# Two of the turns in an attention step leave TensorE: gated values by way of DRAM, exponentials by sixteen small DMAs, each finished by a VectorE transpose

## What is computed

```python
z = cumlogsumexp(s, axis=time)
g = exp(z_prev - z); p = exp(s - z)
hk = hk * g + k[:, None] * p                 # per token, key state
ok = q @ hk                                  # 64 scores of a token and head
pv = softmax(ok)
hv = hv * g[:, None] + p[:, None] * v        # value state
o  = pv @ hv                                 # 128 values of a token and head
o  = o * rsqrt(mean(o*o) + 1e-5) * g_norm_weight
o  = o * (gate * sigmoid(gate))              # the gated values
y  = o.reshape(b, t, VALUE_DIM) @ Wo
```

## Time and profile before

| | |
|---|---|
| time, median of 3 runs | 1524.1 us (1523.93 to 1524.8) |
| the profiled execution | 1523.6 us; its span from first to last instruction 1521.8 us |
| TensorE matmul | 1490.4 us busy, 98% |
| VectorE | 1030.9 us busy, 68% |
| ScalarE, GpSimd | 654.6 us (43%), 432.4 us (28%) |
| granted TensorE clock, mean | 0.997 of full speed |
| DMA | 121.17 MB, mean 80 GB/s; packets under 2 KB 75136 of 108016 |

### The profile page before, as it was taken

The page is one execution under the profiler, slowest core; times in us unless marked ns, Lnnn a source line. Parts: engine busy times, 40 slices in busy tenths (PEclk is TensorE's granted clock), DMA queues, the critical chain, the costliest instruction groups (busy, mean ns, idle before and its releaser), DMA issues.

```text
span 1521.8 us, 24247 instructions
## 1 busy us (share of the span) xinstructions
PE 1490.4 (98%) x9586; PEld 1207.6 (79%) x9586; DVE 1030.9 (68%) x1992; ACT 654.6 (43%) x1249; POOL 432.4 (28%) x282
## 2 busy tenths in 40 slices
PE   8999999999999999999999999999999898999998
PEld 6888888888888888888888888878878655666676
DVE  5666655665556666655666577777777776877788
ACT  5333333333323333333443333334333357677675
POOL 0211011210204344433454433122331333333320
PEclk9999999999999999999999999999999999999999
DMA  4421111110202121222223311101200315444553
GB/s 154 167 63 56 42 49 56 58 67 29 75 17 69 60 82 63 83 70 70 84 85 98 88 53 49 47 25 39 63 30 27 111 70 171 127 132 132 160 168 97
DMA packets 108016, 121.17 MB, mean 80 GB/s; under 512 B 5376, under 2 KB 75136, under 8 KB 107904
## 3 DMA queue, kind: packets, MB, share of 16 engines
q1 hardware_dynamic: 103920, 113.07, 23.5%
q10 hardware_dynamic: 3984, 6.56, 1.2%
HBM read 92.34 MB, written 27.26 MB: 79 GB/s over the span
## 4 chain that ended last, share of the span: by engine, by line
PE 92%; DVE 4%; issue 1%; ACT 1%; POOL 1%; DMA 0%; POOLq 0%; DVEq 0%; ACTq 0%
PE bank L457 19%; PE bank L463 18%; PE bank L460 18%; PE bank L686 6%; PE bank L583 4%; PE bank L701 4%; PE bank L722 3%; PE bank L545 2%; PE bank L518 2%; PE bank L591 2%; PE bank L569 2%; PE bank L526 1%; PE bank L540 1%; PE bank L533 1%; PE bank L577 1%
## 5 line engine op out<-in xcount | busy, mean ns | idle before, releaser
L457 PE MATMUL bank<-Wh,X 128*128 128x512 f32 x512 | 210.5, 411 | 0.3 <-ACT Kt L830 0.2
L463 PE MATMUL bank<-Wh,X 128*128 128x512 f32 x512 | 201.0, 392 | 0.0
L460 PE MATMUL bank<-Wl,X 128*128 128x512 f32 x512 | 199.8, 390 | 0.0
L824 ACT ACTIVATE V<-bank 128x256 f32<-128x256 f32 x128 | 49.0, 383 | 317.3 <-PE bank L463 317.3
L1425 POOL TENSOR_TENSOR sm<-sm,half 128x8 f32<-128x8 f32 x32 | 52.7, 1648 | 391.7 <-DVE sm L1127 391.7
L457 PE MATMUL bank<-X,Wh 128*128 128x512 f32 x384 | 157.1, 409 | 6.6 <-ACT Wh L779 6.1
L460 PE MATMUL bank<-X,Wh 128*128 128x512 f32 x384 | 151.0, 393 | 0.0
L1407 POOL TENSOR_TENSOR Wl<-RAW,Wh 128x512 fp32r<-128x512 f32 (+1 forms) x65 | 112.4, 1738 | 135.6 <-ACT Wh L779 135.6
L463 PE MATMUL bank<-X,Wl 128*128 128x512 f32 x384 | 150.8, 393 | 0.0
L1448 POOL TENSOR_TENSOR LO<-M,HI 128x512 fp32r<-128x512 f32 x64 | 81.9, 1280 | 165.9 <-PE bank L695 106.4
L686 PE MATMUL bank<-XT,W 128*128 128x512 bf16 x512 | 122.8, 383 | 2.9 <-ACT XI L897 2.3
(11 more groups left out here) (213 smaller groups left out, 3313.0 us busy)
## 6 DMA issues: line engine op xcount, KB each, us to landing
z_scratch<-EV SPq DMA_DIRECT2D x64, 256.0 KB, 2.0
Z<-z_scratch SPq DMA_DIRECT2D x16, 1024.0 KB, 5.9
RAW<-wgT SPq DMA_DIRECT2D x16, 512.0 KB, 4.0
RAW<-wuT SPq DMA_DIRECT2D x16, 512.0 KB, 3.8
RAW<-wdT SPq DMA_DIRECT2D x16, 512.0 KB, 3.6
RAW<-Wo SPq DMA_DIRECT2D x14, 512.0 KB, 3.6
RAW<-Wv SPq DMA_DIRECT2D x26, 256.0 KB, 2.9
RAW<-Wg SPq DMA_DIRECT2D x26, 256.0 KB, 3.4
```

What stands on the lines that cost most here:

```text
L457: engine.matmul(o, lh(c), rh(c), start=c == 0, stop=False)
L460: engine.matmul(o, lh(c), rl(c), start=False, stop=False)
L463: last = engine.matmul(o, ll(c), rh(c), start=False, stop=c == n - 1)
```

## The change

The step numbers here are those of the data. `MOVED` is 20.

- **Gated values, steps 0 to 19.** VectorE writes them to `OG` in another column order (`OGB`). SyncE stores `OG` to a DRAM tensor `o_scratch` by four DMAs of 32 partitions each, waits for them, waits for `ok` of the step after, and loads the whole of it (128 x 1024 float32) into `AM`. One VectorE transpose in place (it turns each block of 32 x 32) finishes the turn; ScalarE and VectorE make `OTh` and `OTl` out of `AM` in place of two PSUM banks. The 8 TensorE transposes of these steps are gone.
- **Exponentials, steps 2 to 19.** SyncE issues sixteen DMAs from `ET` to `Et`, each 32 partitions by 4 x 32 float32, and one VectorE transpose in place on `Et` finishes. The 4 TensorE transposes and ScalarE's copy are gone.
- **Order of the loops 0 to 20.** `vg2` stands ahead of `y` rather than between `weights` and `values`; `turn_o` stands after `turn_w`; the last `tern` stands ahead of `keys`. `turn_og` and `turn_e` are the two VectorE transposes. The order of the later loops is as before.
- Some semaphores are merged, their waits go by the sum, and `HOLD` has other numbers for `en`, `xt`, `q`, `sc`, `ok`, `w`, `et` and `x1`, so the banks are dealt out differently in the whole program.

```diff
+MOVED = 20
+
+ALONE = ("states", "q", "tern", "k", "load_x", "ok", "sums", "s", "turn_ok", "vg0", "turn_og", "turn_w", "turn_o", "tern", "vg1", "vg2", "y", "scores", "weights", "turn_e", "values", "tern", "keys", "vg3")
...
@@ tensor, attend
                 elif stage == "turn_o":
+                    if n < MOVED:
+                        return
...
@@ vector
+            def turn(stage, n):
+
+                if stage == "turn_og":
+                    dve.wait_ge(S["ot_in"], 16 * n + 16)
+                    engine.transpose(OTF, OTF).then_inc(S["ot_made"], 1)
+                else:
+                    dve.wait_ge(S["et_in"], 256 * (n - 1))
+                    dve.wait_ge(S["hk_mm"], n)
+                    e = Et[:].rearrange("p i n -> p (i n)")
+                    engine.transpose(e, e).then_inc(S["et_made"], 1)
...
@@ sync
+            def send(stage, n):
+
+                if stage == "o":
+                    sp.wait_ge(S["o_gated"], n + 1)
+                    sp.wait_ge(S["ot_in"], 16 * n)
+                    src = OG[:].rearrange("p h i v -> p (h i v)").rearrange("p (b x) -> p b x", b=4)
+                    to = way.rearrange("(b r) (a x) -> r b a x", b=4, a=4)
+                    for a in range(4):
+                        engine.dma_start(to[:, :, a], src[32 * a:32 * a + 32]).then_inc(S["o_stored"], 16)
+                    sp.wait_ge(S["o_stored"], 64 * (n + 1))
+                    sp.wait_ge(S["ok_sum"], n + 2)
+                    engine.dma_start(OTF, way).then_inc(S["ot_in"], 16)
+                else:
+                    sp.wait_ge(S["e_exp"], n + 1)
+                    sp.wait_ge(S["ok_sum"], n)
+                    sp.wait_ge(S["hv_mm"], n)
+                    src = ET[:, n % 2, :].rearrange("p (i b c) -> p i b c", i=4, b=4)
+                    for a in range(4):
+                        for b in range(4):
+                            engine.dma_start(Et[32 * b:32 * b + 32, :, 32 * a:32 * a + 32],
+                                             src[32 * a:32 * a + 32, :, b, :]).then_inc(S["et_in"], 16)
```

More of the change, by code:

```diff
@@ L50, in wait_ge @@
             self.engine.wait_ge(sem, value)
-ALONE = ("states", "q", "tern", "k", "load_x", "ok", "sums", "s", "turn_ok", "turn_o", "vg0", "tern", "turn_w", "vg1",
-         "y", "scores", "weights", "vg2", "values", "keys", "tern", "vg3")
+MOVED = 20
+ALONE = ("states", "q", "tern", "k", "load_x", "ok", "sums", "s", "turn_ok", "vg0", "turn_og", "turn_w", "turn_o", "tern", "vg1", "vg2", "y", "scores", "weights", "turn_e", "values", "tern", "keys", "vg3")
 STEP = ("states", "q", "k", "tern", "load_x", "ok", "sums", "turn_o", "s", "turn_ok", "vg0", "turn_w", "tern", "vg1",
         "y", "vg2", "scores", "weights", "values", "keys", "tern", "vg3")
-OF_NEXT = ("q", "k", "s", "vg0", "vg1", "vg2", "vg3", "keys", "scores")
+OF_NEXT = ("q", "k", "s", "vg0", "vg1", "vg2", "vg3", "keys", "scores", "turn_e")
 def step_order(n, tasks):
@@ L75, in step_order @@
                 yield stage, n + 2
-        elif 0 <= m < STEPS:
+        elif (2 if stage == "turn_e" else 0) <= m < (MOVED if stage in ("turn_og", "turn_e") else STEPS):
             yield stage, m
@@ L108, in attention_order @@
 def attention_order():
-    for stage in OF_NEXT:
+    for stage in OF_NEXT[:9]:
         yield stage, 0
@@ L272, in build @@
         zs = nc.dram_tensor("z_scratch", (NB, 16, 128, T), F).ap()
+        way = nc.dram_tensor("o_scratch", (128, 1024), F).ap()
         IDN, ONE = C[:, 0, :], C[:, 2, :]
@@ L505, in attend @@
                     mm.then_inc(S["k_turned"], 1)
+                    if 1 < n < MOVED:
+                        return
+                    be = take(("et", n), (S["et_made"], n + 1))
+                    pe.wait_ge(S["e_exp"], n + 1)
                     for i in range(4):
@@ L1357, in attention @@
                     project(stage, n)
+                elif stage in ("turn_og", "turn_e"):
+                    turn(stage, n)
                 else:
@@ L1486, in context @@
                                  ).then_inc(S["ctx_in"], 16)
+            def send(stage, n):
[9 more added lines that the diff above has]
+                    engine.dma_start(OTF, way).then_inc(S["ot_in"], 16)
+                else:
+                    sp.wait_ge(S["e_exp"], n + 1)
[6 more added lines that the diff above has]
+                                             src[32 * a:32 * a + 32, :, b, :]).then_inc(S["et_in"], 16)
+            sends, freed, until = [], {}, -1
+            for place, (stage, n) in enumerate(attention_order()):
+                if stage == "q" and 2 <= n < MOVED + 2:
+                    sends.append((place, "o", n - 2))
+                if stage == "s" and 1 < n < MOVED:
+                    sends.append((place, stage, n))
+                if stage == "tern" and (n < 24 or 27 <= n < 51):
+                    freed["F", n // 27, n % 27 // 8, n % 27 % 8] = place
+                elif stage == "load_x":
+                    freed["x", n, 0] = freed["x", n, 1] = place
+                elif stage != "tern" and stage not in CROSS:
+                    for key in new_weights(stage, n):
+                        freed[key] = place
             held = {}
@@ L1490, in sync @@
             for no, (key, where, loop) in enumerate(pieces):
+                if no == 16:
+                    for b in range(NB):
+                        engine.dma_start(Y[:, 4 * b:4 * b + 4, :],
+                                         x[b].rearrange("(i p) d -> p i d", p=128)).then_inc(S[f"y_in{b}"], 16)
+                until = max(until, freed.get(held.get(where), -1))
+                while sends and sends[0][0] < until:
+                    send(*sends.pop(0)[1:])
                 if no == 9:
@@ L1542, in sync @@
                                      wd[kind][:, :, 128 * hp:128 * hp + 128]).then_inc(done, 16)
+            for _, stage, n in sends:
+                send(stage, n)
             sp.wait_ge(S["ctx_lo_g"], 2)
```

99 lines of the change are left out of this document (58 added, 41 removed).

## The result

| | before | after |
|---|---|---|
| time, median (4 runs each) | 1524.01 us (1523.88 to 1524.8) | 1504.05 us (1503.13 to 1506.39) |
| ratio, 95% interval | | 0.987 (0.9853 to 0.9887) |
| the profiled execution, its span | 1523.6, 1521.8 us | 1503.13, 1501.3 us |
| granted TensorE clock, mean | 0.997 | 0.998 |

A forecast was written before the change was run, and what follows sets the result against it. TensorE was taken to bound loops 0 to 20, so removed work counts one for one: -24.9 for transposes, +1.0 for order, +1.5 for late loads, -22.4 in all, giving 1501.7 us; range 1497 to 1519.

The forecast's parts named there:

- What is removed: TensorE, early loops: dropping OG and ET transposes saves 0.86 and 0.43 us each loop, 17.2 and 7.7, together -24.9 us.
- The new order: Loops 0 to 20: values behind weights waits for VectorE's mask, nearly paid by one saved switch; +0.05 a loop, +1 us.
- VectorE: Between vg0 and the masks: y and the mask wait on VectorE's chain; both covered with some 0.35 us to spare.
- T: Length of VectorE's transpose of 1024 columns in AM: taken as 1.25 us, bounds 0.6 and 2.4, limit 1.6 before y waits.
- a sum of -6: Total instead of -24 if the skill's scaled 2.5 us transpose held, y then waiting 0.9 us a loop.
- Rival B: VectorE bounds the moved loops, through a dear transpose or late load into AM: 1506 to 1519 us, chance 0.17.
- The way of the gated values: Stores and load into AM through SyncE: slack 1.2 us, some lateness in five loops with new weights; +1.5 us in all.
- The exponentials: Sixteen DMAs to Et at 0.41 us an issue, all landed before VectorE's transpose; slack 5 to 7 us, cost nothing.
- rival D: SyncE can't issue the sixteen DMAs in time, TensorE stops at states past 1.05 us each; slower, e.g. 1545 us, chance 0.09.
- The bank table: New PSUM bank numbers, whole program: can only change waits for PSUM, +-3.6 us, taken as 0.
- Sum: Whole kernel: -24.9 + 1.0 + 1.5 = -22.4 us; profiled execution 1501.2, median 0.5 above it, 1501.7 us.
- case A: Whole kernel: the forecast holds, with small waits; 1498 to 1506 us, chance 0.66.

The follow-up runs named there:

- exponentials alone: Changed kernel with only the exponentials of steps 2 to 19 moved, gated values turned on TensorE in every step: ratio 0.9975, median 1520.0 us.
- gated values alone: Changed kernel with only the gated values of steps 0 to 19 moved, exponentials turned on TensorE in every step: ratio 0.9943, median 1514.5 us.
- the order alone: Changed kernel with its loop order, merged semaphores and bank table, but both turns back on TensorE in every step: ratio 1.0017, median 1526.0 us.
- the doubled transpose: Changed kernel with the VectorE transpose of AM made twice in a row, leaving the gated values unturned: 1524.2 us (one execution).
- the doubled DMAs: Changed kernel with sixteen more DMAs of the same shape per step to a spare DRAM tensor, Et's transpose waiting for all 32: 1615.2 us (one execution).
- an "earlier" place: Changed kernel with the gated values' stores issued at the place of values and the load into AM at that of ok: ratio 0.9996.

## Why the prediction was right, and where it was off

**What is removed: right.** 0.43 and 0.86 us a loop were forecast. 34.80 against 35.22 (exponentials alone) and 34.37 against 35.22 (gated values alone) give 0.42 and 0.85. Distances between block starts, not the transposes' own busy time, were the right price.

**The new order: right in kind, too small.** +0.05 a loop and +1 us were forecast; the order alone measured +0.08 to 0.14 a loop and +1.8. `values` 2.83 us behind `scores` with 0.30 of idle time is exactly the late loop's figure. That `vg2` in its new place saves a switch was right too; the term was mis-sized by 0.8 us.

**VectorE: right.** T is 1.24 against 1.25 taken, and `y` doesn't wait in the common loops. The cover there was 0.5 to 0.6 us, not 0.35. The choice between 0.6 and 2.4 by the reduction's row held: this transpose reads and writes 1024 columns in the time of one pass. The Trainium skill (VectorE: DVE Perf Modes, the three transpose paths) gives 311 ns for 128x128 bf16; scaled by squares, an estimate, it had made 2.5 us and a sum of -6 (-4.4 with the +1.5 of the late loads, which that sentence of the prediction leaves out). The trace disagrees with that scaling by a factor of two: 1.24 us for eight such squares of float32, 0.70 for four. The measurement decides. Rival B's mechanism is real, as the doubled transpose shows, but it begins 0.6 us above T in the loops whose load is in time.

**The way of the gated values: right in kind, mis-sized.** +1.5 us was forecast for late loads, in the loops with new weights. They are late there (VectorE idle 1.36 and 1.08 us in loops 18 and 19; in six more the load is late by 0.17 to 0.88) because in the queue a weight load that waits for GpSimd's `Wl` stands ahead of the stores:

```profile
679.35 0.37 SPq L1630 DMA_DIRECT2D RAW<-Ws  x1
679.82 1.93 SPq L1545 DMA_DIRECT2D o_scratch<-OG  x4
683.95 0.34 SPq L1548 DMA_DIRECT2D AM<-o_scratch  x1
...
687.44 1.25 DVE L1073 STREAM_TRANSPOSE AM<-AM 128x1024 f32<-128x1024 f32 x1 [1.36 <-DMA AM<-o_scratch]
...
691.32 0.19 PEld L473 LDWEIGHTS bank<-Woh,OTh 128*128 128x128 f32 x1 [0.90 <-DVE OTl L1188]
```

In all the gated values bring 2.6 us less than their transposes took, where I had 1.5. `y`'s waits are nearly all of it: 2.3 us in four loops of the changed kernel, 2.4 us in five with the gated values alone.

**The exponentials: right, by more luck than the text admits.** No wait for `Et` appears, and landing is 1.9 us. But the price of an issue, 0.41 us by the earlier trace rows, was wrong: sixteen took 10.27 us, 0.64 each (652.08 to 662.35), over half as much again. In this loop weight loads stand ahead of them in the queue, one of which waits, and they start 4.7 us after the end of `s` (at 647.38); the last lands at 663.6, and VectorE comes to the transpose at 665.54, a slack of 2.0 us. Over the 18 loops the slack goes from 1.6 to 5.1, where I had 5 to 7, and 2.8 less with loads ahead. A slip in a sum helped to hide it: 541.43 + 1.29 - 526.54 - 0.86 + 2.73 is 18.05, not 17.05, and 18.16 was measured; by its own terms the forecast was 6 to 8.

The limit of 1.05 us an issue that I gave for rival D goes by TensorE alone. VectorE comes first: it had 2.0 us in hand at the transpose and 1.56 idle behind it, 3.5 in all or 0.22 by DMA, so by this estimate it would run late from about 0.86 an issue where loads stand ahead. No run places the limit; the doubled DMAs went far past both figures and cost 112 us. With 0.64 measured where I had 0.41, D was nearer than its 0.09.

The Trainium skill (DMA: Bandwidth & Descriptors, Rules for kernel authors) says to coalesce transfers under 64 KB. Sixteen 16 KB DMAs and one store with four 64 KB loads gave the same time here (1504.05 and 1503.72), since both are under cover. What the small ones cost is issue time on SyncE, 0.64 us each; the 1.9 us from issue to landing of one overlap with those of the next, since all sixteen are in 11.5 us after the first is issued.

**The bank table: right**, nothing.

**Sum.** With the order's 1.8 and the 2.6 in place of the forecast's 1.0 and 1.5: -17.2 - 7.7 + 1.8 + 2.6 = -20.5, and the span fell by 20.5. That it closes is no further proof, since the 2.6 was itself taken as what is missing from 17.2. The forecast was -22.4; 0.8 of the difference is the order, 1.1 the late loads. The profiled execution was to be 1501.2 and was 1503.13; the median of the runs lies 0.9 above it, where I had carried over 0.5 from before. 1504.05 is 2.3 us above the forecast of 1501.7, and is case A. Part of the hit is luck: what was mis-sized for the DMAs fell into slack that happened to be there.

## What to carry to other kernels

Where TensorE is the bound, work taken off it counts one for one, but only if the engines that take it over are given cover: here an equally long block (`vg2`) had to be put ahead of the product that uses the result, and without it the same change is 2% slower. Price a transfer by three numbers, the issue on its queue, the landing, and above all what stands ahead of it in that queue: an "earlier" place behind an instruction that waits cost the whole gain. And look for the limit of a rival at every in-order engine that must wait, with the idle time behind that wait, not at the last user of the data alone.

## What was not expected of the hardware

**The distance of two issues depends on the DMA's shape.** SyncE's issues of 256 KB weight loads stand 0.41 us apart; those of 16 KB with 32 partitions by 4 runs of 128 bytes stand 0.64 us apart, and the four loads of 64 KB, of runs of 128 bytes too, take 0.70 each (2.82 us).

**GpSimd's clip and VectorE's scan lengthen each other, by how they meet.** GpSimd's clip of 128 x 1024 took 3.63 us in every loop before, and VectorE's scan 1.21 to 1.22. After, the clip takes 4.66 in six loops, and in two others the scan takes 2.06:

```profile
655.75 4.66 POOL L1464 TENSOR_SCALAR RAW<-RAW 128x1024 f32<-128x1024 f32 x1 [4.69 <-ACT RAW L822]
...
655.77 1.22 DVE L1097 TENSOR_TENSOR_SCAN ZT<-C,ET 128x512 f32<-128x512 f32 x1
...
485.17 3.65 POOL L1464 TENSOR_SCALAR RAW<-RAW 128x1024 f32<-128x1024 f32 x1 [7.30 <-ACT RAW L822]
485.25 2.06 DVE L1097 TENSOR_TENSOR_SCAN ZT<-C,ET 128x512 f32<-128x512 f32 x1
...
691.51 4.32 POOL L1464 TENSOR_SCALAR RAW<-RAW 128x1024 f32<-128x1024 f32 x1 [6.49 <-ACT RAW L822]
```

It doesn't come with the moved data. With order alone, where nothing is moved and `OTl` reads a PSUM bank, the clip is 3.63 everywhere but the scan takes 1.66 to 1.73 us in nine loops, and the same with the exponentials alone:

```profile
464.25 3.63 POOL L1465 TENSOR_SCALAR RAW<-RAW 128x1024 f32<-128x1024 f32 x1 [17.89 <-ACT RAW L823]
464.64 1.72 DVE L1098 TENSOR_TENSOR_SCAN ZT<-C,ET 128x512 f32<-128x512 f32 x1
```

What goes with it is the lead of the clip over the scan. With a lead of 0.98 us (the kernel before) both have their own length. With 0.39 to 0.45 the scan takes 1.66 to 1.73, and with 0.08 to 0.09 it takes 2.06: in both cases it ends some 2.1 us after the clip's start. With a lead of 0.02 the scan keeps its 1.22 and the clip takes 4.66, and a clip that begins 0.33 us into the scan (691.51) takes 4.32: both end 3.4 us after the scan. (Once, with `vg2` put back, a lead of 0.03 went the other way: the scan took 2.08.) So one of the two keeps its length and the other is put off, and with a lead of 0.98 neither is. The Trainium skill (SBUF — State Buffer, SBUF: two separate sides) describes a pair of ports that VectorE and GpSimd share as a lock held for a whole instruction, which a VectorE operation with two SBUF inputs needs against a GpSimd one that reads SBUF. The trace fits it where the scan begins first, and where the two begin almost together. Where the clip has a longer lead it doesn't: in the kernel before, the scan ran in 1.21 us wholly under a clip that had begun 1.0 us ahead of it, so the clip did not shut it out for its whole length. No run here isolates the cause. The effect cost no time that I can find.
